# Expert tiles in one table and two lists, weight splits and scales inside attention, last rows routed among the tiles

## Chip, cores and metric

The kernel runs on one core of a Trainium2 chip. The metric is device time in microseconds (us) of one execution. The engines are TensorE (PE, with its weight loads PEld), VectorE (DVE), ScalarE (ACT), GpSimd (POOL) and SyncE (SP), each with an instruction queue of its own that runs in order; they wait for one another by semaphores.

## What is computed

The input is one image x of shape 1 x 64 x 128 x 128. First an attention block with a residual, then a mixture of experts with a residual:

```python
x = x + conv_ref(_ln_c(x), ...)          # per-pair layer norm, attention over the last axis, gate, projection
t = tokens(x)                            # 8192 tokens of 128 features
t = t + ffn_ref(_ln_t(t), ...)

# conv_ref: x = (x - mu) * rsqrt(var + eps) * ln_w + ln_b   (mean and variance over everything)
#   q, k, v, g = projections of 4 heads of 32; softmax(q k / sqrt(32) + bias) v, times sigmoid(g), times wrep
# ffn_ref: gate_logits = xf @ Wg + bg; top 2 of 8 experts, weights by a softmax over the two
for e in range(E):
    h = gelu(xf @ W1[e] + b1[e])         # 128 -> 512
    out = out + w_dense[:, e:e + 1] * (h @ W2[e] + b2[e])
```

The kernel computes an expert only for the tokens that chose it.

## The kernel before

The image lies in SBUF as 64 rows (HALF) of 128 tokens each: the partition is the channel and half, a row is a slice xt[:, i, :]. Three phases follow each other.

**Prologue.** SP and ACT each load one half: the x chunks, then the four chunks of ln_w, then the four of ln_b (`load_half`, L524 to L535). DVE computes row statistics in two chains of two chunks, prepares the projection weights (L925 to L934), gets the global scale, and multiplies and adds ln_w and ln_b chunk by chunk (L943, L949). PE computes the bias of attention from x1 (`bias_rows`, L1281) and transposes it.

**Attention.** 32 units of four rows run in a software pipeline of 35 steps (`attention_steps`, `step(s, p)` on every engine). Unit u is projected in step u, its logits and exponentials follow in steps u and u+1, its values in step u+2, its residual (L1011) in step u+3. The order on each engine is written out by hand. The routing of finished rows rides along: `plan()` says in which step statistics, row scales, normalised rows (POOL), transposes, gate logits (PE), picks and ranks of a batch happen. BATCHES are rows 0 to 15, 16 to 27, 28 to 39 and 40 to 63; only the first three are routed inside attention. POOL scatters each routed row of 128 tokens by an indirect DMA (L700), once for each of two choices, into a region per expert in HBM. `scatter_plan()` gives it at most 5 a step, 8 after step 31; twelve of batch 2 are left for after attention. ACT squares the expert weights in steps 32 and 33 (`weight_squares`, L824); DVE builds the first tile table in step 33 (`tile_table`).

**Between attention and tiles.** PE sums the squares (L1446), DVE gets the power-of-two scales (L1180 to L1190), then does statistics, scales and rows of batch 3 (L1061), b2 (L1197 to L1202), its logits, picks, ranks, positions and the second table, and two `split_weights` (L1207). ACT makes the high parts of the weights (L864), copies turned rows (L814) and the 24 late rows (L869). PE waits for table 2 and both splits before it starts the tile steps.

**Tiles.** The table has 78 tiles of 256 tokens in two parts: 2 * 40 * 128 / 256 + 7 = 47 for rows 0 to 39, and 31 for rows 40 to 63. A tile that isn't full is filled by padding rows, which SP writes (`pad_rows`) into the regions. SP loads a tile (`load_rows`, L589), eight buffers ahead. In step s PE transposes tile s+1 (L1473), multiplies tile s by W1 (L1483 to L1485, hidden layer in fp16 high and low parts), and tile s-1 by W2 (L1500). ACT makes fx_h, the Gelus (L887) and the weighted output yo of tile s-2 (L895). DVE makes the low parts (L1226) and the hidden high and low parts (L1232, L1234). POOL sends a tile with two indirect DMAs (L728). ACT may write yo of tile t only when tile t-4 is sent. Among the sends of the first 38 tiles POOL also scatters the 48 late rows. From step 54 on DVE adds first results to xt (`add_first`, L1248) in every second step. The steps 5 to 52 run in a loop of eight.

The lines that the steps below touch in PE's tile step, before:

```python
pe.wait_ge(table_ready, 2)
pe.wait_ge(w_split, 2)
tile_steps(pe, tile_step)
```

## Time and profile before

| | |
|---|---|
| median of 3 runs | 893.18 us |
| lowest, highest | 892.15, 895.83 us |
| profiled execution | 893.04 us, its span 891.3 us |
| PE / PEld / DVE busy | 77% / 63% / 73% of the span |
| ACT / POOL busy | 69% / 45% |
| mean granted clock of PE | 0.906 |
| HBM traffic | 70 GB/s over the span |

The span runs from the first to the last instruction; the device time has 1.7 us more. A line of the trace names the source line, the engine, the operation and out<-in, with a count and times. "idle before" is the engine's idle time just before, and what ended it. DMAs of a queue are issued in order and land later.

### The profile page before, as it was taken

What the parts mean: (1) busy time and instruction counts of PE and PEld (TensorE: products, weight loads), DVE (VectorE), ACT (ScalarE), POOL (GpSimd) and SP (SyncE); (2) the same over time, 40 slices, a digit from 0 to 9 for tenths busy, and PEclk for the clock granted to TensorE, in tenths of its full rate; (3) what the DMA queues carried; (4) which work ended last, traced back from release to release, by engine and by line L of the source; (5) the groups of instructions that cost most, each with busy time, mean ns of one, the idle gap of its engine ahead of it and who ended that gap; (6) DMA issues with size and microseconds to landing.
All of it is one profiled execution on the core that took longest, in us unless ns stands there. A gap on an engine that the chain in (4) does not pass through costs nothing.

```text
span 891.3 us, 23217 instructions
## 1 busy us (share of the span) xinstructions
PE 686.5 (77%) x7225; PEld 559.9 (63%) x7226; DVE 650.3 (73%) x2359; ACT 615.3 (69%) x1548; POOL 405.4 (45%) x469
## 2 busy tenths in 40 slices
PE   0089999997996889678977635299888888999980
PEld 0088777775775667557856425278666766888860
DVE  3983688887778667877677584778666766799974
ACT  0862899996996669568866652078766676888860
POOL 5000122223433256346553760047777777666661
PEclk9999999998998879879988755599999999999995
DMA  9959200000000001000100132113333223434457
GB/s 215 259 124 201 56 3 2 2 2 1 2 2 2 1 16 32 4 7 26 32 26 16 46 88 57 43 50 82 90 83 86 84 81 93 154 97 143 150 159 256
DMA packets 65923, 63.98 MB, mean 72 GB/s; under 512 B 21157, under 2 KB 57062, under 8 KB 64296
## 3 DMA queue, kind: packets, MB, share of 16 engines
q1 hardware_dynamic: 54168, 34.90, 15.9%
q0 software_dynamic: 9152, 18.76, 6.3%
q10 hardware_dynamic: 2512, 9.18, 3.8%
q8 instruction: 48, 0.79, 0.4%
q14 instruction: 43, 0.35, 0.1%
HBM read 35.88 MB, written 26.93 MB: 70 GB/s over the span
## 4 chain that ended last, share of the span: by engine, by line
PE 51%; DVE 17%; ACT 9%; POOL 8%; issue 7%; DMA 6%; SPq 1%; ACTq 0%; POOLq 0%; DVEq 0%
PE PT L1500 8%; PE PT L1338 6%; ACT L L801 5%; POOL expert_out L728 5%; DMA shared<-in_L_conv_ln_b 4%; PE B L1368 4%; PE S L1326 4%; POOL routed L700 3%; PE S L1483 3%; PE B L1281 3%; PE S L1485 3%; PE S L1484 3%; PE A L1293 2%; DVE xt L1011 2%; DVE pl L976 2%
## 5 line engine op out<-in xcount | busy, mean ns | idle before, releaser
L728 POOL DMA_INDIRECT expert_out<-yo,rows_all x156 | 157.4, 1009 | 87.1 <-ACT yo L895 49.7
L887 ACT ACTIVATE hf<-S,b_sb,inv_hscale 128x256 f32<-128x256 f32 x312 | 150.9, 564 | 47.4 <-PE S L1485 46.8
L801 ACT ACTIVATE L<-L,lmin 128x128 f32<-128x128 f32 x512 | 159.4, 392 | 0.4
L700 POOL DMA_INDIRECT routed<-pay,pos x128 | 125.1, 977 | 69.9 <-issue 34.6
L989 DVE CUSTOM_DVE_ANT_0 L<-S,biasN 128x128 f32<-128x128 f32 x512 | 117.3, 284 | 16.3 <-issue 15.1
L684 POOL TENSOR_TENSOR og<-on,rden 128x256 f32<-128x256 f32 x64 | 39.4, 617 | 193.0 <-DVE on L1002 134.1
L1234 DVE SCALAR_TENSOR_TENSOR hl<-hf,hscale,hh 128x512 f16<-128x512 f32 x156 | 117.8, 755 | 5.5
L1232 DVE TENSOR_SCALAR hh<-hf,hscale 128x512 f16<-128x512 f32 x156 | 77.5, 497 | 54.0 <-ACT hf L887 53.9
L1483 PE MATMUL S<-fx_h,w_h 128*128 128x256 f16 x312 | 86.8, 278 | 11.1 <-issue 9.5
L796 ACT ACTIVATE ph<-PT 128x512 f16<-128x512 f32 x128 | 75.9, 595 | 25.5 <-PE B L1355 16.8
L1338 PE MATMUL PT<-identity,L 128*128 128x128 f32 x512 | 81.7, 296 | 10.1 <-ACT L L801 10.0
L976 DVE TENSOR_TENSOR pl<-PT,ph 128x512 f16<-128x512 f32 x128 | 84.2, 683 | 6.3 <-ACT ph L796 6.0
L1500 PE MATMUL PT<-w_h,hh 128*128 x624 | 86.6, 220 | 2.1 <-DVE hl L1234 1.8
L672 POOL TENSOR_TENSOR xs<-x,xs 64x512 fp32r<-64x512 f32 x32 | 40.6, 1268 | 103.4 <-ACT xs L777 67.1
L1484 PE MATMUL S<-fx_l,w_h 128*128 128x256 f16 x312 | 86.5, 277 | 0.0
L1485 PE MATMUL S<-fx_h,w_l 128*128 128x256 f16 x312 | 86.4, 277 | 0.0
L1500 PE MATMUL PT<-w_h,hl 128*128 x624 | 85.8, 219 | 0.0
L1500 PE MATMUL PT<-w_l,hh 128*128 x624 | 85.7, 219 | 0.0
L1326 PE MATMUL S<-qk_all 32*128 32x128 f32 x1024 | 78.2, 293 | 0.7 <-ACT qk_all L783 0.7
L1293 PE MATMUL A<-xs,w4h 128*128 128x512 f32 x64 | 46.0, 718 | 38.7 <-DVE vl L970 37.6
L1338 PEld LDWEIGHTS PT<-identity,L 128*128 128x128 f32 x512 | 62.9, 152 | 17.9 <-ACT L L801 12.2
L1326 PEld LDWEIGHTS S<-qk_all 32*128 32x128 f32 x1024 | 65.5, 195 | 8.1 <-issue 5.7
(238 smaller groups left out, 1738.4 us busy)
## 6 DMA issues: line engine op xcount, KB each, us to landing
rows_all<-routed SPq DMA_DIRECT2D x78, 130.0 KB
shared<-expert_out SPq DMA_DIRECT2D x6, 768.0 KB
shared<-in_L_ffn_W SPq DMA_DIRECT2D x8, 512.0 KB, 7.2
routed<-blank SPq DMA_DIRECT2D x30, 129.0 KB, 2.6
expert_out<-yo,rows_all POOLq DMA_INDIRECT x156
out<-xt SPq DMA_DIRECT2D x6, 384.0 KB
xt<-in_x SPq DMA_DIRECT2D x4, 512.0 KB, 14.3
xt<-in_x ACTq DMA_DIRECT2D x4, 512.0 KB, 9.8
```

Of the source, the lines that this page charges most:

```text
L700: pool.indirect_dma_start(routed[TABLE_OF[b]], bass.IndirectOffsetOnAxis(ap=pos[k][:, row:row + 1], axis=0), source[:, part_row(b, i), :], ...
L728: pool.indirect_dma_start(expert_out, bass.IndirectOffsetOnAxis(ap=row_place[t % IN_BUFS][:, k, W + 1:W + 2], axis=0), yo[t % YO_BUFS][:, ...
L801: last = nc.scalar.activation(L[p][:, h, i, :], L[p][:, h, i, :], ACT.Exp, scale=-1.0, bias=lmin[p][:, h * R + i:h * R + i + 1])
L887: last = nc.scalar.activation(hf[p][:, b, :], S[2 * p + pair][:, k * TILE:(k + 1) * TILE], ACT.Gelu, scale=inv_hscale[:, 0:1], bias=b1_fla ...
L989: last = nc.vector.tensor_tensor_reduce(out=L[p][:, h, i, :], in0=S[h][:, i * P:(i + 1) * P], in1=biasN[:, h, :], scale=-float(D) ** -0.5, ...
L1234: nc.vector.scalar_tensor_tensor(hl[p][:, b, :], hf[p][:, b, :], hscale[:, 2:3], hh[p][:, b, :], ALU.mult, ALU.subtract).then_inc(hl_ready, 1)
L1326: last = nc.tensor.matmul(S[h][:, c], q[d, c], k[d, c], start=True, stop=True)
L1338: last = nc.tensor.transpose(PT[i % 2][:, h * P:(h + 1) * P], L[p][:, h, i, :], identity[:])
L1483: nc.tensor.matmul(dst, w1_h[:, block_at], fx_h[p][:], start=True, stop=False)
L1484: nc.tensor.matmul(dst, w1_h[:, block_at], fx_l[p][:], start=False, stop=False)
L1485: last = nc.tensor.matmul(dst, w1_l[:, block_at], fx_h[p][:], start=False, stop=True)
L1500: last = nc.tensor.matmul(PT[p][:, k * P:(k + 1) * P], h_part[p][:, b, k * P:(k + 1) * P], w_part[:, block_at], start=False, stop=b == HB ...
```

## The change

- One table with 71 tiles replaces two tables with 78. It has two lists of eight experts: the tiles of rows 0 to 39 and those of rows 40 to 63, with one region per expert, so that late rows go on where the routed ones end. FULL = 33 tiles are sure to be full, and need neither padding nor the late rows. `full_table` (DVE, step 33) gives these 33; `rest_table_counts`, `rest_table` and `rest_table_rows` give the other 38 in tile steps 11 to 13.
- ACT squares the weights in eight blocks, two in each of the steps 17 to 20 (`SQUARES_STEP`); b1's square is made in step 24; PE sums them and DVE reads and makes the scales in step 25 (`SCALES_STEP`). ACT makes the high parts in steps 32 and 33, DVE the low parts in steps 33 and 34.
- PE, ACT and DVE start the tile steps once table 1 is there. In the tile steps come b2 (after step -1), row scales (0), late rows (1 to 3), their turns (2 to 7) and logits (3 to 8), picks (8, 9), ranks and positions (10). POOL scatters the 48 late rows from tile 8 to tile 28, SP pads the regions before load 29, and loads tile 33 once all is scattered.
- All tile steps are written out, no loop. The additions of first results come in two of three steps, from step 52.
- Scatters in attention: 6 a step, 8 in steps 22 to 24, 28 to 30 and after 31; second choices one step sooner.
- Prologue: ln_w and ln_b chunks are loaded in turns; three chains of row scales (chunk 0, chunk 1, chunks 2 and 3); weight preparation on ACT and POOL; the first product with ln_w ahead of the global scale.

```diff
+    ROUTED = sum(n for _, n in BATCHES[:3])
+    FULL = ROUTED - (E - 1)
+    TILES = 2 * HALF * P // TILE + E - 1
...
+        ADD_AT = {DONE + 5 + 3 * i // 2: divmod(i, 4) for i in range(12)}
...
+        SQUARES_STEP, SCALES_STEP = 17, 25
+        LATE_STEP = dict(rows=1, turns=2, picks=8, ranks=10)
...
-                quota = 5 if s < UNITS else 8
+                quota = 14 if s == LAST - 1 else 8 if s in (22, 23, 24, 28, 29, 30) or s >= UNITS else 6
...
             for c in range(CH):
                 engine.dma_start(lnw_at[c][k], lwv[f, :, chunk(c), :]).then_inc(lnw_in[c], 16)
-            for c in range(CH):
                 engine.dma_start(lnb_at[c][k], lbv[f, :, chunk(c), :]).then_inc(lnb_in[c], 16)
...
+            load_rows(0, FULL - IN_BUFS // 2)
+            pad_regions()
+            load_rows(FULL - IN_BUFS // 2, FULL)
+            sp.wait_ge(padded, 32 * PADS)
+            sp.wait_ge(table_ready, 2)
+            for k in range(2):
+                sp.wait_ge(scattered[3][k], 16 * BATCHES[3][1])
+            load_rows(FULL, DONE + IN_BUFS)
...
-            spread = PART_TILES[0] - 9
+            start, spread = LATE_STEP["ranks"] - 2, FULL - 4 - (LATE_STEP["ranks"] - 2)
...
+                if 0 <= s - SQUARES_STEP < HB:
+                    weight_squares(2 * (s - SQUARES_STEP))
+                    weight_squares(2 * (s - SQUARES_STEP) + 1)
+                if s in (UNITS, UNITS + 1):
+                    high_weights(s - UNITS)
...
+            def copy_late():
+                act.wait_ge(xn_ready, GROUPS)
+                nc.scalar.activation(pay[2][:, :, 0:W], pay[1][:, :, 0:W], ACT.Copy).then_inc(copied, 1)
...
+            tile_steps(tile_step, {LATE_STEP["turns"] + 1: copy_late, LATE_STEP["ranks"]: lambda: gate_exponential(3)})
...
+                if s == SCALES_STEP - 1:
+                    bias_squares()
+                if s == SCALES_STEP:
+                    weight_scales()
                 if s == UNITS + 1:
-                    tile_table(0, carry[3])
+                    full_table()
+                    split_weights(0)
+                if s == UNITS + 2:
+                    split_weights(1)
...
+            after = {-1: second_bias, 0: lambda: scale_rows(3), picked: lambda: pick(3, (0, 1)), picked + 1: lambda: pick(3, (2, 3)),
+                     placed: lambda: positions(3), placed + 1: rest_table_counts, placed + 2: lambda: held.extend(rest_table()),
+                     placed + 3: lambda: rest_table_rows(*held)}
+            for n in range(3):
+                after[LATE_STEP["rows"] + n] = lambda n=n: late_normal_rows(ROUTED // R + 2 * n, ROUTED // R + 2 * n + 2)
...
+                    if turned_at(s) - 1 in LATE_GROUPS:
+                        gate_logits(turned_at(s) - 1, S[2 * p + 1], 0)
+                    if turned_at(s) in LATE_GROUPS:
+                        turn_rows(turned_at(s), S[2 * p], pay[1])
+                    if s == LATE_STEP["ranks"]:
+                        rank(3, S[2 * p + 1], 0)
...
-            pe.wait_ge(table_ready, 2)
-            pe.wait_ge(w_split, 2)
-            tile_steps(pe, tile_step)
+            pe.wait_ge(table_ready, 1)
+            tile_steps(tile_step, {})
```

## Rows read from the trace of the kernel before

**Rows 1.** Busy us (x instructions) by stretch: PE, PEld, DVE, ACT, POOL; clock, DMA.
```profile
200.00:507.00 307.00, 246.56 (x2665) 197.29 (x2663) 228.33 (x1145) 229.23 (x610) 143.03 (x165) 0.88 0.05 15
507.00:575.00 68.00, 27.39 (x164) 21.89 (x163) 48.20 (x157) 19.29 (x16) 21.39 (x23) 0.53 0.24 60
575.00:742.60 167.60, 148.21 (x1615) 118.17 (x1616) 117.10 (x210) 119.51 (x292) 117.20 (x121) 0.97 0.29 80
742.60:857.00 114.40, 113.08 (x1329) 95.62 (x1327) 100.64 (x179) 95.84 (x237) 75.36 (x72) 1.00 0.45 137
```

**Rows 2.** Timeline (start us, us, what): PE's transposes of tiles 0 and 43.
```profile
574.95 0.45 PE L1473 MATMUL A<-identity,rows_all 128*128 128x128 f32 x1 [15.23 <-issue]
...
742.60 0.28 PE L1473 MATMUL B<-identity,rows_all 128*128 128x128 f32 x1
```

**Rows 3.** Timeline: POOL's first send of a tile.
```profile
588.62 0.96 POOL L728 DMA_INDIRECT expert_out<-yo,rows_all  x1 [21.09 <-ACT yo L895]
```

**Rows 4.** Timeline: VectorE in the prologue.
```profile
36.69 0.20 DVE L925 COPY gt<-bgrow 1x128 f32<-1x128 f32 x1
...
38.97 1.39 DVE L934 TENSOR_TENSOR w4l<-og,w4h 64x512 fp32r<-64x512 f32 x2
...
46.33 2.48 DVE L949 SCALAR_TENSOR_TENSOR x<-x,grstd,shared 128x1024 f32<-128x1024 f32 x2 [1.33 <-DMA shared<-in_L_conv_ln_b]
```

**Rows 5.** DMA issues by line, 8.15 to 8.30 us: KB each, us to landing.
```profile
shared<-in_L_conv_ln_w SPq DMA_DIRECT2D x1, 512.0 KB, 25.9
```

**Rows 6.** Timeline: ScalarE between steps 18 and 19.
```profile
295.36 2.44 ACT L801 ACTIVATE L<-L,lmin 128x128 f32<-128x128 f32 x8
297.70 0.37 ACT L789 ACTIVATE gt<-A 128x256 f32<-128x256 f32 x1
```

**Rows 7.** Groups by line and form, ScalarE, 498 to 517 us: busy, mean ns, idle before.
```profile
L824 ACT ACTIVATE w_h<-shared 128x4096 f16<-128x4096 f32 x2 | 7.2, 3606 | 0.0
```

**Rows 8.** Timeline: the residual, once a step, of steps 22, 23 and 32 to 34.
```profile
350.47 0.76 DVE L1011 SCALAR_TENSOR_TENSOR xt<-B,brep,xt 64x512 f32<-64x512 f32 x1 [1.01 <-PE B L1368]
365.81 0.74 DVE L1011 SCALAR_TENSOR_TENSOR xt<-B,brep,xt 64x512 f32<-64x512 f32 x1 [1.90 <-PE B L1368]
...
494.72 0.76 DVE L1011 SCALAR_TENSOR_TENSOR xt<-B,brep,xt 64x512 f32<-64x512 f32 x1 [0.50 <-PE B L1368]
509.37 0.74 DVE L1011 SCALAR_TENSOR_TENSOR xt<-B,brep,xt 64x512 f32<-64x512 f32 x1 [1.59 <-PE B L1368]
520.28 0.76 DVE L1011 SCALAR_TENSOR_TENSOR xt<-B,brep,xt 64x512 f32<-64x512 f32 x1
```

**Rows 9.** Timeline: first table, a weight split, SyncE's first eight loads.
```profile
514.26 0.16 DVE L1152 TENSOR_TENSOR counts<-carry,region_base 128x8 f32<-128x8 f32 x1
...
557.31 4.48 DVE L1207 SCALAR_TENSOR_TENSOR w_l<-shared,hscale,w_h 128x4096 f16<-128x4096 f32 x1
...
539.38 8.43 SPq L589 DMA_DIRECT2D rows_all<-routed  x8
```

**Rows 10.** Chain that ended last, 660 to 672 us: start us, us, what.
```profile
665.50 2.24 DMA expert_out<-yo,rows_all
...
668.46 2.34 DMA rows_all<-routed
...
670.84 0.44 PE A L1473 x2
```

**Rows 11.** Groups by line and form, VectorE, 740 to 857 us: the additions of results.
```profile
L1248 DVE SCALAR_TENSOR_TENSOR xt<-shared,y_scale,xt 128x768 f32<-128x768 f32 x11 | 11.1, 1011 | 0.0
```

**Rows 12.** Busy us by stretch, columns as rows 1: scales and rows; picks; ranks, positions.
```profile
525.90:536.35 10.45, 4.66 (x20) 3.85 (x20) 9.79 (x45) 7.64 (x4) 8.01 (x9) 0.50 0.35 92
552.50:557.40 4.90, 0.04 (x1) 0.05 (x2) 4.44 (x15) 0.42 (x1) 0.00 (x0) 0.50 0.00 0
561.70:565.80 4.10, 0.00 (x0) 0.00 (x0) 3.65 (x17) 0.00 (x0) 0.00 (x0) 0.50 0.00 0
```

**Rows 13.** Timeline: ScalarE at the first Gelu.
```profile
578.35 1.28 ACT L887 ACT_TABLE_LOAD   x1 [1.89 <-PE S L1485]
```

More of the change, by code:

```diff
@@ L592, in _, with pad_rows @@
-            pad_regions(0)
-            sp.wait_ge(padded[0], 32 * PADS)
+            def pad_rows(at, n):
+                where = routed[at].rearrange("(k p) w -> p k w", p=P)
+                sp.dma_start(where[:, :, 0:W + 1], blank[:]).then_inc(padded, 16)
+                sp.dma_start(where[:, :, W + 1:W + 2], pad_place[:, n, :].bitcast(F32).unsqueeze(2),
+                             allow_slow_non_contiguous=True).then_inc(padded, 16)
+            for n in range(E - 1):
+                pad_rows(slice(E * REGION + n * TILE, E * REGION + (n + 1) * TILE), E + n)
@@ new lines, in pad_regions, with load_rows @@
+            def pad_regions():
+                sp.wait_ge(counts_ready, 1)
+                for e in range(E):
+                    at = sp.value_load(count_at[0:1, e:e + 1], min_val=0, max_val=TOKENS)
+                    pad_rows(bass.ds(at + e * REGION, TILE), e)
+            def load_rows(first, stop):
+                for t in range(first, stop):
+                    wait(sp, y_sent[t % YO_BUFS], sent_count(t % YO_BUFS, t - IN_BUFS))
+                    at = sp.value_load(row_at[0:1, t:t + 1], min_val=0, max_val=E * REGION + (E - 2) * TILE)
+                    sp.dma_start(rows_in[t % IN_BUFS], routed[bass.ds(at, TILE)].rearrange("(k p) w -> p k w", p=P)
+                                 ).then_inc(rows_loaded[t % IN_BUFS], 16)
@@ L908, in _, with multiply_weights @@
             chain = Chain(dve, dve_step)
-            for b in range(2):
-                for c in (2 * b, 2 * b + 1):
+            def multiply_weights(c):
+                dve.wait_ge(rows_normal, c + 1)
+                dve.wait_ge(lnw_in[c], 32)
+                nc.vector.tensor_tensor(x1[:, chunk(c), :], x1[:, chunk(c), :], lnw_at[c], ALU.mult).then_inc(lnw_used, 1)
+            for first, stop in ROW_CHAINS:
+                for c in range(first, stop):
                     dve.wait_ge(x_in[c], 32)
@@ L914, in _ @@
                 chain.link(last)
-                k = slice(2 * b * CR, 2 * (b + 1) * CR)
+                k = slice(first * CR, stop * CR)
                 row_scales(chain, k, 1e-6)
@@ L1111, in positions @@
                 first, n = BATCHES[b]
-                rows, t = slice(first, first + n), TABLE_OF[b]
+                rows = slice(first, first + n)
                 a, c, f = r_a[:, 0:n, :], r_b[:, 0:n, :], posf[:, 0:n]
@@ L1209, in split_weights, with second_bias, late_normal_rows @@
                                                w_h[n][:].rearrange("p b e d -> p (b e d)"), ALU.mult, ALU.subtract).then_inc(w_split, 1)
-            for g in range(10, GROUPS):
-                take_logits(g, B)
-            pick(3)
-            split_weights(0)
-            take_ranks(3, B)
-            positions(3)
-            tile_table(1, carry[4])
-            split_weights(1)
+            attention_steps(step)
+            def second_bias():
+                dve.wait_ge(hscale_ready, 1)
+                chain.link(nc.vector.tensor_scalar(b2_row[:], b2_row[:], hscale[0:B2_ROWS, 1:2], hscale[0:B2_ROWS, 2:3], ALU.mult, ALU.mult))
+                b2_e = b2_row[:].rearrange("o (e d) -> o e d", e=E)
+                chain.link(nc.vector.tensor_copy(b2_parts[:], b2_e))
+                lo = slice(B2_ROWS - 1, B2_ROWS)
+                chain.link(nc.vector.tensor_tensor(b2_parts[lo], b2_e[lo], b2_parts[lo], ALU.subtract))
+                nc.vector.tensor_copy(ones_x[:], ones[0:B2_ROWS, :]).then_inc(b2_ready, 1)
+            def late_normal_rows(first, stop):
+                for g in range(first, stop):
+                    normal_rows(g)
             def tile_step(s, m, _=None):
@@ L1384, in gate_logits, with rank @@
                 for i in range(R):
-                    last = nc.tensor.matmul(bank[:, RANK_AT + i * E:RANK_AT + (i + 1) * E], xnT[:, i * P:(i + 1) * P], wg_sb[:],
+                    last = nc.tensor.matmul(bank[:, column + i * E:column + (i + 1) * E], xnT[:, i * P:(i + 1) * P], wg_sb[:],
                                             start=True, stop=True)
                 last.then_inc(lg_full, 1)
-            def rank(b, bank):
+            def rank(b, bank, at=RANK_AT):
                 n = BATCHES[b][1]
```

435 lines of the change are left out of this document (232 added, 203 removed).

## Prediction

> **What bounds the kernel now.** I read the stage table first [rows 1]: each engine's busy time by stretch. In the last 35 tiles TensorE is busy 113 of 114 us, but only 27 of the 68 us between 507 and 575, at a mean granted clock of 0.53: there weights are squared, scaled and split and rows 40 to 63 are routed, and no tile is computed. The first tile's transposes start at 574.95, those of tile 43 at 742.60 [rows 2]. Between them TensorE isn't the bound either: from the first send at 588.62 [rows 3] POOL issues 121 indirect DMAs in 154 us [rows 1], 1.27 us each without a rest, since the scatter of every late row (48) and every tile's two sends cost that much. The last 35 tiles and the tail take 891.3 - 742.6 = 148.7 us and change little. So four places are to be priced: prologue, attention, gap, and the tiles up to the last late scatter.
>
> **Prologue: -5 us.** VectorE does 3.7 us of weight preparation (36.69 to 40.36) ahead of its global statistic, then one product, then waits 1.33 us for the first ln_b chunk, until 46.33 [rows 4]. The change gives the preparation to ScalarE and POOL, which idle there, and issues ln_b 0 where ln_w 1 stands now: near 8.2, in 25.9 us [rows 5], so it lands at 34.1. First output of L949: 46.33 moves to about 41.3, and the small matmuls behind it with it. The third chain of row scales ends before it is needed: nothing.
>
> **Attention: +13.1 us.** (a) The squares move from steps 32 and 33 into steps 17 to 20, two blocks a step. In place of them come the scaled copies, as long: no gain there. ScalarE is tight where they are put: it ends eight exponentials begun at 295.36 and starts the gate at 297.70 without idle time [rows 6], and VectorE's chain hangs on the copy behind that gate. An operation of 128x4096 takes 3.61 us [rows 7], a quarter of it 0.90, with its fixed part and accumulator read 1.15, two a step 2.3. The step that carries a square today took 509.37 - 494.72 = 14.7 us, the next 10.9 [rows 8]: 3.8 for 3.8. Exposed: 4 x 2.0 = 8; bounds 0 and 10. (b) Scales in step 25: eleven chained VectorE operations of 0.2 us. A step with six pick operations took 365.81 - 350.47 = 15.3 us [rows 8], 4.4 over a plain one, more than the chain's own length, as TensorE idles and restarts slow. +3; bounds 1 and 4.4. (c) A matmul and its read in bank A, and b1's square: +0.8; bounds 0 and 1.5. (d) Scatters 6 and 8 a step for 5: in steps 25 to 27 POOL also normalises rows; one scatter, 1.27, comes through, and later steps have fewer: +1.3; bounds -1 and 4. With the prologue attention ends 8.1 later than now.
>
> **The gap: the first tile 21.8 us earlier.** VectorE's table starts at 514.26 and the residual behind it at 520.28 [rows 8, 9]: 6.0 us, now 4.5 with 33 entries for 47. Then the first weight split, 4.5 [rows 9], which the change puts ahead of the last residual and second choice (1.2 us). Second choice ends at 524.9, not 521.5: 3.4 later. Then, as now, 12 scatters and the loads at 539.38 [rows 9]: with 3.4 and 8.1, 550.9. Transposes start 2.3 us behind a load [rows 10]: 553.2. The second split hides behind the scatters. The padding of the regions leaves this path, as the first 33 tiles are full.
>
> **Tiles 0 to 32: the work of the gap comes back.** The late rows now go between tiles on VectorE. A plain tile costs it (100.6 - 11.1) / 34.8 = 2.6 us [rows 1, 11] of TensorE's 3.3, which leaves 0.7. Until the late positions are known (after step 10) it does: 5.7 us to the first hidden block, as now, which covers b2's four operations; 11 tiles, 28.3; row scales and 24 rows 10.45; logits 1.2; picks 4.9; ranks and positions 4.1 [rows 12]. Sum 54.7. Its waits: in steps 4 to 8 TensorE takes 3.3 + 1.4 for four fp32 transposes and the logits, against 2.8 on VectorE, 9.5 in all; partly at the same time ScalarE's copy of 24 rows, queued ahead of tile 5's fx_h, on which TensorE waits; rank matmuls 2.2; one restart at the half clock 1.1. The positions are ready 67.5 us after tile 0: 620.7. Bounds 58 and 73.
>
> POOL's first late scatter stands ahead of send 8 and waits for the positions with send 8 behind it, and ScalarE's output 12 waits for send 8. Then 48 scatters and sends 8 to 27: 88 x 1.27 = 111.8 us, to 732.5. Only then may SyncE load tile 33. From a POOL DMA at 665.50 to the transposes of the tile whose load waited for it it's 5.4 us [rows 10]: tile 33 at 737.9. TensorE, some six tiles ahead of the sends, runs dry about 10 us before. 38 tiles remain, where 35 remain at 742.60: 737.9 + 148.7 + 3 x 3.3 = 896.5, and +1.5 as the additions of first results, 1.01 us [rows 11], come in two of three tiles instead of one of two: 2.6 + 0.67 = 3.3, no room left. Span 898.0. The profiled run took 893.04 for its span of 891.3, the median is 893.18: with 1.7, 899.7, taken as 899.5. Seven tiles of 3.3 and the gap are gained, but 33 tiles now cover 185 us where 43 covered 168.
>
> The Exp of the late rows' gate stands between Gelus. The first Gelu's table load takes 1.28 us [rows 13], so two more cost ScalarE 2.6 in step 10, beside VectorE's ranks: about 0.5 on the path, inside the 67.5. The Trainium skill (ScalarE: Activation LUTs, What ACT_TABLE_LOAD costs) puts a switch at about 2.7 us with its drain, 5.3 for two, and so speaks against this placement.
>
> **Rivals.** (1) Faster: squares and scales hide in attention, where ScalarE is busy 229 of 307 us [rows 1]. Against it: the tight place above. If attention costs 2 for 13, and ScalarE's copy and the turned rows hide behind VectorE's own work (4.5): 899.5 - 11 - 4.5 = 884. It decides whether ScalarE comes to the gates of steps 18 to 21 with over 2 us in hand. (2) Half of it: (a) and (b) cost 6 for 11, the copy 2 less: 892.5. (3) The clock: each time TensorE runs dry (steps 2 and 10, before tile 33) it restarts at 1.2 GHz, as at 575; three restarts at 2 us more than counted, and 1 us in each square step: +10, 909. The 0.97 of that stage now [rows 1] speaks against. (4) Each of the two switches also empties ScalarE, for about the load's own length, in the one step where hidden blocks, ranks and gate meet: 2 x 1.28, so 902. This is what the skill's figure gives; the row has one load behind an idle time, and can't tell. That the tiles don't start at once is no case: table, first split and high parts are ready over 15 us before the loads.
>
> **Chances.** Forecast 0.42, of which 0.07 within the bound; (1) 0.25; (2) 0.12; (3) 0.13; (4) 0.08. A measurement can tell about 0.5%, 4.5 us, from no change. Faster 0.25; same 0.07 + 0.12 = 0.19; slower 0.35 + 0.13 + 0.08 = 0.56. The range goes from 881, rival (1) with its terms' lower bounds, to 910, rival (3); the forecast's own is 893 to 905.
>
> **What would show it.** Right: the first bias matmul near 42.7; steps 17 to 20 each 2 us longer and step 25 by 3; the first tile's transposes near 553; the last late scatter near 732, 180 us behind it; TensorE idle some 10 us before tile 33; then 3.3 us a tile. Wrong: steps 17 to 20 no longer than now (rival 1), a granted clock under 0.9 from tile 0 to 32 (rival 3), or a POOL that has pauses among the late scatters.

## The result, and the profile of the changed kernel

| | before | changed |
|---|---|---|
| median of 5 runs | 892.15 us | 905.33 us |
| lowest, highest | 890.92, 895.83 us | 905.00, 911.12 us |
| ratio of the changed to before | | 1.0151, 95% interval 1.013 to 1.0171 |
| profiled execution | span 891.3 us | 911.12 us, span 908.6 us |
| first tile's transposes | 574.95 | 557.10 |
| first, last late scatter | | 630.97, 742.99 |
| transposes of tile 33, from there to the end | | 748.79, 159.8 |

The kernel got slower by 1.5%. The direction is the one forecast (slower had a chance of 0.56), the size isn't: 899.5 against 893.2 us was 6.3 us more, and the medians differ by 13.2. By time alone the rivals at 902 and 909 us lie nearer to 905.3 than the forecast does, so only the rows can choose. The changed kernel's trace is of the slowest of its five executions (granted clock 0.883); the other four took 905.0 to 905.5 us with spans near 903.2 (0.897 to 0.901). About 5 us of what follows belong to that one execution, and I say where.

Stretches of the changed kernel, columns as in [rows 1]: attention, gap, tiles up to the first late scatter, late scatters, the last 37 tiles.

```profile
105.00:515.00 410.00, 335.94 (x3652) 269.39 (x3651) 302.40 (x1545) 322.24 (x855) 169.88 (x196) 0.89 0.04 13
515.00:557.00 42.00, 8.33 (x65) 4.25 (x64) 19.09 (x40) 5.99 (x5) 16.74 (x14) 0.54 0.07 22
557.00:631.00 74.00, 59.00 (x548) 49.47 (x549) 51.79 (x141) 42.59 (x91) 16.61 (x17) 0.85 0.16 43
631.00:749.00 118.00, 76.03 (x778) 59.41 (x777) 66.80 (x136) 57.65 (x143) 90.24 (x92) 0.85 0.28 82
749.00:870.00 121.00, 120.61 (x1393) 101.89 (x1393) 104.06 (x186) 100.34 (x248) 72.50 (x70) 0.98 0.41 123
```

In the third stretch POOL is busy 16.6 of 74 us: the engine that is the bound afterwards has nothing to do, since the positions aren't known. In the fourth it issues without a rest and TensorE works 76 of 118 us. Timeline of the prologue (start us, us, what):

```profile
40.81 2.48 DVE L973 SCALAR_TENSOR_TENSOR x<-x,grstd,shared 128x1024 f32<-128x1024 f32 x2
...
42.24 3.98 PE L1380 MATMUL B<-wb_sb,x 128*128 128x8 f32 x18 [5.21 <-DVE x L973]
```

46.33 [rows 4] has become 40.81 without a wait for ln_b. The gap: VectorE's two weight splits, POOL's first scatters of the last batch in attention, and TensorE's first tile:

```profile
527.49 4.46 DVE L1286 SCALAR_TENSOR_TENSOR w_l<-shared,hscale,w_h 128x4096 f16<-128x4096 f32 x1
...
533.07 4.48 DVE L1286 SCALAR_TENSOR_TENSOR w_l<-shared,hscale,w_h 128x4096 f16<-128x4096 f32 x1
...
533.44 4.98 POOL L719 DMA_INDIRECT routed<-pay,pos  x1 [9.71 <-DVE pay L1176]
538.73 0.96 POOL L719 DMA_INDIRECT routed<-pay,pos  x1 [0.30 <-issue]
...
557.10 0.66 PE L1567 MATMUL A<-identity,rows_all 128*128 128x128 f32 x2 [29.43 <-DMA rows_all<-routed]
```

The first scatter meets the second split and takes 4.98 us instead of 0.96; it ends 0.87 us behind the split (533.07 + 4.48 = 537.55). Next, the largest stall among the first tiles, between tiles 6 and 7 (584.7 to 597.8), on ScalarE and TensorE:

```profile
584.02 2.77 ACT L898 ACTIVATE pay<-pay 128x3072 f32<-128x3072 f32 x1 [4.07 <-DVE pay L1094]
586.70 0.36 ACT L906 ACTIVATE fx_h<-B 128x256 f16<-128x256 f32 x1
...
589.61 0.28 PE L1587 MATMUL S<-fx_h,w_h 128*128 128x256 f16 x1 [4.50 <-ACT xnT L837]
```

ScalarE waits 4.07 us for the last of the late rows, copies them for 2.77, and only then turns to fx_h and the turned rows that TensorE waits for. Last, the chain from the last late scatter to tile 33 (start us, us, what), and TensorE's row for it:

```profile
742.99 2.30 DMA routed<-pay,pos
...
746.48 2.27 DMA rows_all<-routed
748.79 0.69 PE B L1567 x2
...
748.79 0.69 PE L1567 MATMUL B<-identity,rows_all 128*128 128x128 f32 x2 [10.78 <-DMA rows_all<-routed]
```

### The profile page after: what moved, and what is told of

The parts are those of the page before. It is cut to its first block, busy times and chain, and to the rows that moved or that the text cites. A ratio compares the mean times of both kernels' runs of the same rounds, so it can differ in the third digit from the quotient of the medians.

```text
span 908.6 us, 21702 instructions
## 1 busy us (share of the span) xinstructions
PE 674.0 (74%) x6950; PEld 549.3 (60%) x6950; DVE 630.6 (69%) x2346; ACT 601.3 (66%) x1514; POOL 400.0 (44%) x450
## 3 DMA queue, kind: packets, MB, share of 16 engines
q1 hardware_dynamic: 44104, 31.97, 13.9%
## 4 chain that ended last, share of the span: by engine, by line
PE 46%; DVE 23%; ACT 10%; issue 7%; POOL 6%; DMA 5%; SPq 2%; ACTq 0%; POOLq 0%; DVEq 0%
PE PT L1613 7%; PE PT L1439 6%; ACT L L824 5%; PE B L1469 4%; POOL routed L719 4%; PE S L1427 3%; PE B L1380 3%; PE S L1587 3%; PE S L1589 2%; PE S L1588 2%; PE A L1392 2%; DVE xt L1035 2%; DVE hl L1325 2%; POOL expert_out L747 2%; DVE pl L1000 2%
## 5 line engine op out<-in xcount | busy, mean ns | idle before, releaser
L747 POOL DMA_INDIRECT expert_out<-yo,rows_all x142 | 144.9, 1020 | 118.2 <-ACT yo L927 87.6
L917 ACT ACTIVATE hf<-S,b_sb,inv_hscale 128x256 f32<-128x256 f32 x284 | 137.9, 565 | 44.3 <-PE S L1589 44.3
L824 ACT ACTIVATE L<-L,lmin 128x128 f32<-128x128 f32 x512 | 159.8, 392 | 0.5
L1013 DVE CUSTOM_DVE_ANT_0 L<-S,biasN 128x128 f32<-128x128 f32 x512 | 117.3, 285 | 17.7 <-issue 16.5
L1325 DVE SCALAR_TENSOR_TENSOR hl<-hf,hscale,hh 128x512 f16<-128x512 f32 x142 | 107.0, 754 | 5.1
L1587 PE MATMUL S<-fx_h,w_h 128*128 128x256 f16 x284 | 82.0, 289 | 15.2 <-DVE fx_l L1313 8.2
L1323 DVE TENSOR_SCALAR hh<-hf,hscale 128x512 f16<-128x512 f32 x142 | 69.7, 491 | 32.3 <-ACT hf L917 32.1
L1613 PE MATMUL PT<-w_h,hh 128*128 x568 | 80.5, 224 | 5.0 <-DVE hl L1325 4.7
L1589 PE MATMUL S<-fx_h,w_l 128*128 128x256 f16 x284 | 81.9, 288 | 0.0
L1588 PE MATMUL S<-fx_l,w_h 128*128 128x256 f16 x284 | 81.9, 288 | 0.0
L1439 PEld LDWEIGHTS PT<-identity,L 128*128 128x128 f32 x512 | 64.3, 155 | 26.5 <-ACT L L824 20.6
L1613 PE MATMUL PT<-w_h,hl 128*128 x568 | 80.0, 223 | 0.0
L1613 PE MATMUL PT<-w_l,hh 128*128 x568 | 79.8, 223 | 0.0
## 6 DMA issues: line engine op xcount, KB each, us to landing
xt<-in_x SPq DMA_DIRECT2D x4, 512.0 KB, 14.2
```

The source lines that it names most:

```text
L747: pool.indirect_dma_start(expert_out, bass.IndirectOffsetOnAxis(ap=row_place[t % IN_BUFS][:, k, W + 1:W + 2], axis=0), yo[t % YO_BUFS][:, ...
L824: last = nc.scalar.activation(L[p][:, h, i, :], L[p][:, h, i, :], ACT.Exp, scale=-1.0, bias=lmin[p][:, h * R + i:h * R + i + 1])
L917: last = nc.scalar.activation(hf[p][:, b, :], S[2 * p + pair][:, k * TILE:(k + 1) * TILE], ACT.Gelu, scale=inv_hscale[:, 0:1], bias=b1_fla ...
L1013: last = nc.vector.tensor_tensor_reduce(out=L[p][:, h, i, :], in0=S[h][:, i * P:(i + 1) * P], in1=biasN[:, h, :], scale=-float(D) ** -0.5, ...
L1325: nc.vector.scalar_tensor_tensor(hl[p][:, b, :], hf[p][:, b, :], hscale[:, 2:3], hh[p][:, b, :], ALU.mult, ALU.subtract).then_inc(hl_ready, 1)
L1439: last = nc.tensor.transpose(PT[i % 2][:, h * P:(h + 1) * P], L[p][:, h, i, :], identity[:])
```

## The experiments

All ran beside the kernel before; a ratio is to that, with its 95% interval, and a difference in us is a difference of ratios times 893. The other columns are from the traces, in us: the last residual of attention, the first tile's transposes, the first late scatter, tile 33's transposes.

| kernel | ratio | interval | residual | tile 0 | late | tile 33 | span |
|---|---|---|---|---|---|---|---|
| changed | 1.0151 | 1.0130-1.0171 | 532.0 | 557.1 | 631.0 | 748.8 | 908.6 |
| e1 | 1.0104 | 1.0077-1.0130 | 528.4 | 546.8 | 618.2 | 736.7 | 895.9 |
| e2 | 1.0123 | 1.0100-1.0146 | 527.0 | 548.0 | 623.7 | 742.7 | 901.8 |
| e3 | 1.0083 | 1.0047-1.0119 | 523.5 | 548.6 | 621.0 | 739.6 | 899.2 |
| e4 | 0.9928 | 0.9903-0.9953 | 516.2 | 570.9 | | | 886.8 |
| e5 | 1.0043 | 1.0027-1.0059 | 527.8 | 552.8 | 617.6 | 736.6 | 896.1 |
| e6 | 1.0076 | 1.0050-1.0102 | 526.8 | 551.8 | 624.0 | 736.2 | 895.5 |
| e7 | 0.9912 | 0.9894-0.9930 | 529.7 | 548.0 | 613.1 | 726.3 | 885.4 |
| e8 | 1.0126 | 1.0107-1.0145 | 529.6 | 554.7 | 624.2 | 742.5 | 902.2 |
| e9 | 0.9827 | 0.9793-0.9861 | 524.5 | 542.7 | 605.7 | 718.0 | 877.4 |
| e10 | 0.9817 | 0.9787-0.9846 | 527.8 | 539.9 | 603.2 | 715.7 | 873.5 |
| e11 | 0.9722 | 0.9694-0.9749 | 523.8 | 531.9 | 595.4 | 708.2 | 866.4 |
| e12 | 0.9700 | 0.9676-0.9723 | 519.7 | 527.6 | 591.1 | 703.8 | 863.7 |

e4 has the old order of tiles, so its last columns stay empty. From tile 33 to the end it is 158 to 160 us in all the others: what moves tile 33 moves the time. Steps of attention: column s is the time from the residual in step s to the residual in step s + 1.

| step | 17 | 18 | 19 | 20 | 24 | 25 | 26 | 27 | 28 | 29 | 31 | 33 |
|---|---|---|---|---|---|---|---|---|---|---|---|---|
| before | 20.0 | 15.8 | 18.8 | 11.9 | 15.7 | 11.7 | 13.3 | 11.7 | 15.9 | 15.2 | 10.2 | 10.9 |
| changed | 21.7 | 17.7 | 20.6 | 13.6 | 17.3 | 17.7 | 11.7 | 11.9 | 15.8 | 15.2 | 10.2 | 14.0 |
| e3 | 21.6 | 15.5 | 19.2 | 11.7 | 17.7 | 16.7 | 11.7 | 11.9 | 14.3 | 15.2 | 10.5 | 13.9 |
| e6 | 21.7 | 17.7 | 20.5 | 13.6 | 16.4 | 17.4 | 11.8 | 11.9 | 15.4 | 13.5 | 10.3 | 13.9 |
| e8 | 21.7 | 17.2 | 18.9 | 13.6 | 16.4 | 11.5 | 16.2 | 11.7 | 14.2 | 15.1 | 12.1 | 14.0 |
| e9 | 20.0 | 15.7 | 18.8 | 11.8 | 17.3 | 17.7 | 11.7 | 11.9 | 15.9 | 15.2 | 10.2 | 14.5 |
| e12 | 20.0 | 15.5 | 18.9 | 11.7 | 16.4 | 11.6 | 13.6 | 12.8 | 15.3 | 13.5 | 11.7 | 14.1 |

**e1: the second choice one step earlier.**

```diff
-  second_at.setdefault(min(s + 1, LAST - 1), []).append(b)
+  second_at.setdefault(min(s + 1, LAST - 2), []).append(b)
```

> The changed kernel with one move: the second choice of rows 28 to 39 (two VectorE operations that wait for POOL's first twelve scatters, issued by 513.1 in the changed kernel) stands at the end of step 33 instead of step 34, ahead of the table, the first weight split and the last residual. Theory (the chain second choice, twelve scatters, load sets the first tile, and each weight split holds up the one POOL scatter that meets it): the scatters begin near 523.8 instead of 533.4, two of them take about 5 us instead of 0.96, the last ends near 547 instead of 552.3, the first tile's transposes stand near 552 instead of 557.1, and the time falls by 5 us, to about 900. Rival A (the slow first scatter is a cost of its own, not of the split): only one takes 5 us, the first tile stands near 548, -9. Rival B (something else, weights or the table, sets the first tile): the scatters move and the first tile doesn't, 0.

Measured: -4.2 us; its interval touches that of the changed kernel. POOL's scatters of the last batch:

```profile
523.70 0.96 POOL L719 DMA_INDIRECT routed<-pay,pos  x1 [0.30 <-issue]
524.97 4.27 POOL L719 DMA_INDIRECT routed<-pay,pos  x1 [0.30 <-issue]
529.54 4.99 POOL L719 DMA_INDIRECT routed<-pay,pos  x1 [0.30 <-issue]
534.84 0.95 POOL L719 DMA_INDIRECT routed<-pay,pos  x1 [0.30 <-issue]
```

Two slow scatters, one for each split (splits 523.93 to 528.39 and 529.22 to 533.70), and none that is slow for being the first: rival A falls. The scatter at 523.70, begun 0.23 us ahead of the first split, took its 0.96. Tile 0 comes 18.4 us behind the last residual instead of 25.1, so rival B falls too.

**e2: the second split among the tiles.**

```diff
-                if s == UNITS + 2:
-                    split_weights(1)
...
                 nc.vector.tensor_copy(ones_x[:], ...).then_inc(b2_ready, 1)
+                split_weights(1)
```

> The changed kernel with the second weight split moved from behind the second choice to a place behind the first tile's low part and the second bias, where VectorE waits for the first hidden block. Theory (the split held POOL's first scatter for 4 us): that scatter takes 0.96 us, the loads come 4 us earlier, the first tile's transposes stand near 553 as first forecast; of the 4.5 us that the split now takes between tiles 0 and 1 about 2 are exposed, so the time falls by 2 (between -4 and +1). Rival (the scatter is slow by itself): the first tile stays at 557 and the time rises by 2 to 4.

Measured: -2.5 us. The first scatter took its plain time, and the split stands where VectorE waited:

```profile
528.41 1.01 POOL L719 DMA_INDIRECT routed<-pay,pos  x1 [9.70 <-DVE pay L1174]
...
552.87 4.47 DVE L1284 SCALAR_TENSOR_TENSOR w_l<-shared,hscale,w_h 128x4096 f16<-128x4096 f32 x1
```

Tile 0 comes 21.0 us behind the last residual instead of 25.1: the 4.1 us are the split's hold on POOL. From tile 0 to the first late scatter it is 75.8 us, so some of it is given back. The interval of the time touches that of the changed kernel; the rows are clearer than the time.

**e3: two of eight squares.**

```diff
-                if 0 <= s - SQUARES_STEP < HB:
-                    weight_squares(2 * (s - SQUARES_STEP))
-                    weight_squares(2 * (s - SQUARES_STEP) + 1)
+                if s == SQUARES_STEP:
+                    weight_squares(0)
+                    weight_squares(2 * HB - 1)
```

> The changed kernel with two of its eight squares of the weight blocks (the first of W1 and the last of W2, both in step 17); the other six are left out and ones stand for their sums, so the scales of the weights are other powers of two. Theory (ScalarE is tight where they were put, so each square of 1.03 us is exposed by about 0.9): steps 18 to 20 take 17.7 - 1.8, 20.6 - 1.8 and 13.6 - 1.7 us as in the kernel before, step 17 stays at 21.7, time -5.3. Rival 1 of the prediction (they hide in attention, and the longer steps have another cause): 0.

Measured: -6.1 us (interval some 4 wide to each side); steps 18 to 20 lost 2.2, 1.4 and 1.9, together 5.5, and step 17, which kept its two, stayed at 21.6. Two squares cost 1.4 to 2.2 us wherever they stand in these steps. Rival 1 of the prediction falls.

**e4: the kernel before with the new prologue.** The edit is the prologue's part of the diff above (load_half, ROW_CHAINS, the weight preparation on ScalarE and POOL, multiply_weights), put into the kernel before.

> The kernel before with the prologue of the changed one alone: ln_w and ln_b chunks in turns, row scales in three chains, the weight preparation on ScalarE and POOL. Theory: the first residual comes at 105.0 instead of 110.1, everything behind it moves with it, time 892.2 - 5 = 887. Rival (the 5 us are given back where other transfers or POOL's constants set the pace): between -2 and 0.

Measured: 886.29 us, -6.4 us; by the traces the last residual comes 4.1 earlier and the span is 4.5 shorter. The prologue alone beats both kernels.

**e5: the copy of the late rows later.**

```diff
-                    if k == 0 and i == 0:
+                    if k == 1 and i == 0:
                         pool.wait_ge(copied, 1)
...
-            tile_steps(tile_step, {LATE_STEP["turns"] + 1: copy_late, ...
+            tile_steps(tile_step, {LATE_STEP["ranks"] + 2: copy_late, ...
```

> The changed kernel with ScalarE's copy of the 24 late rows moved from behind tile step 3 to behind tile step 12; POOL waits for it ahead of the first scatter of the late rows' second choice instead of ahead of the first late scatter. Theory (the copy waits about 4 us for VectorE's last row, takes 2.8, and fx_h and the turned rows stand behind it, so that TensorE runs dry at tile 7 and restarts at the half clock): the 13.1 us between tiles 6 and 7 become about 6, the first late scatter comes 67 us behind tile 0 instead of 73.9, the time falls by 6 to 7. Rival (VectorE's own work, rows, picks and positions, sets the positions, and the copy lies beside it): the stall shrinks but the first late scatter moves by 2 at most, time -2 to 0.

Measured: -9.6 us by the ratios. Tile 7 follows tile 6 in 4.7 us instead of 13.1, and the first late scatter stands 64.8 us behind tile 0; in the changed kernel and in e1, e3, e6 and e8, which keep the copy, it is 69.5 to 73.9. The granted clock of that stretch differs too, so I compare at like clock: 71.4 us with the copy (e1, 0.88) against 64.8 and 65.0 without (e5 and e7, 0.89), and 69.5 with it (e8, 0.94) against 63.4 without (e10, 0.94). So 6 to 7 us of the path were this one operation, and its rival falls.

**e6: late scatters over fewer tiles, padding in pieces.**

```diff
-            start, spread = LATE_STEP["ranks"] - 2, FULL - 4 - (LATE_STEP["ranks"] - 2)
+            start, spread = LATE_STEP["ranks"] - 2, FULL - 7 - (LATE_STEP["ranks"] - 2)
...
-            load_rows(0, FULL - IN_BUFS // 2)
-            pad_regions()
-            load_rows(FULL - IN_BUFS // 2, FULL)
+            load_rows(0, FULL - 12)
+            for e in range(E):
+                load_rows(FULL - 12 + e, FULL - 11 + e)
+                pad_region(e)
+            load_rows(FULL - 4, FULL)
```

> The changed kernel with the 48 late scatters spread over sends 8 to 25 instead of 8 to 28, and the padding of the eight regions put singly between loads 21 to 29 instead of as one block ahead of load 29. Theory (POOL sets the pace until the last late scatter; tile 33 then needs that scatter and send 25): 84 indirect DMAs of 1.27 us from the first late scatter instead of 88, so tile 33 comes 5 us earlier, the 16.5 us stall at tile 29 goes and costs nothing of its own, time -5. Rival A (the stall at tile 29 is what makes tile 33 late): more than -8. Rival B (TensorE or the loads can't follow): 0.

Measured: -6.7 us; tile 33 stands 112.2 us behind the first late scatter instead of 117.8. In the changed kernel SyncE pads the regions in one block ahead of load 29, from 704.39 on:

```profile
704.39 0.41 SPq L575 DMA_DIRECT2D routed<-blank  x1
...
718.65 0.37 SPq L576 DMA_DIRECT2D routed<-pad_place  x1
719.96 29.35 SPq L594 DMA_DIRECT2D rows_all<-routed  x7
```

That made 16.5 us between the transposes of tiles 28 and 29, here 7.6. It was no cost of its own: the 5.6 us gained are the four DMAs fewer ahead of tile 33 (5.1), and rival A, which wanted more than 8, falls.

**e7: the three together** (e1, e5 and e6).

> The changed kernel with the second choice in step 33, the copy of the late rows behind tile step 12, and the late scatters over sends 8 to 25 with the padding spread among the loads. All three lie one behind the other on the same path by the theory, so they add: -4 (as measured for the first alone), -6.5 and -5, together -15.5 against the changed kernel, about 890, or 0.997 of the kernel before. If one of them only uncovers another limit, the sum falls short: 895 to 900.

Measured: 886.51 us, -21.3 us against the changed kernel, where the three alone add to -20.5, more than the -15.5 expected. They add, as operations one behind the other on one path do.

**e8: the scale chain in step 31.**

```diff
-        SQUARES_STEP, SCALES_STEP = 17, 25
+        SQUARES_STEP, SCALES_STEP = 17, 31
```

> The changed kernel with the matrix product of the square sums, its read and the eleven chained scale operations in step 31 instead of step 25 (b1's square stays in step 24). Theory (the price of 6.0 us in step 25, 1.6 of it given back in step 26, comes partly from what meets there: picks' batch, eight scatters and row normalisation on POOL, whose operations hold up one of the chain for 1.1 us): step 25 goes back to about 11.7, step 31 rises from 10.2 by 3, time -1.5 (0 to -2). Rival (a chain on VectorE costs the same wherever it stands): step 31 rises by 4.5 to 6, time 0.

Measured: -2.2 us, an interval that touches the changed kernel's. The residuals of steps 25 to 27, changed kernel and then e8:

```profile
404.83 0.74 DVE L1035 SCALAR_TENSOR_TENSOR xt<-B,brep,xt 64x512 f32<-64x512 f32 x1 [2.13 <-PE B L1469]
422.57 0.76 DVE L1035 SCALAR_TENSOR_TENSOR xt<-B,brep,xt 64x512 f32<-64x512 f32 x1 [2.77 <-PE B L1469]
434.30 0.74 DVE L1035 SCALAR_TENSOR_TENSOR xt<-B,brep,xt 64x512 f32<-64x512 f32 x1 [0.87 <-PE B L1469]
```

```profile
404.53 0.74 DVE L1035 SCALAR_TENSOR_TENSOR xt<-B,brep,xt 64x512 f32<-64x512 f32 x1 [1.28 <-PE B L1469]
416.04 0.76 DVE L1035 SCALAR_TENSOR_TENSOR xt<-B,brep,xt 64x512 f32<-64x512 f32 x1 [1.02 <-PE B L1469]
432.27 0.74 DVE L1035 SCALAR_TENSOR_TENSOR xt<-B,brep,xt 64x512 f32<-64x512 f32 x1 [0.88 <-PE B L1469]
```

Step 25 is 11.5 again, but step 26 rose from 11.7 to 16.2. Steps 25 and 26 together took 29.5 and now 27.7, against 25.0 before the change; step 31 rose by 1.9. So the chain costs 1.7 in one place and 1.9 in the other, by the traces, and the 2.7 us by which steps 25 and 26 are still over the kernel before belong to something else, the scatters (e12).

**e9: the squares where ScalarE idles.** ScalarE's two longest waits near steps 17 to 24, in e7's trace:

```profile
286.52 0.60 ACT L807 ACTIVATE qk_all<-A 128x512 f32<-128x512 f32 x1 [6.30 <-PE A L1394]
...
381.02 0.21 ACT L843 ACTIVATE gate_e<-key 128x12 f32<-128x12 f32 x1 [5.63 <-DVE key L1129]
```

```diff
                 unit(s, p, 2, high_p, 1)
+                if s == 24:
+                    for j in range(HB, 2 * HB):
+                        weight_squares(j)
...
                 unit(s, p, 1, exponentials, 0)
+                if s == 18:
+                    for j in range(HB):
+                        weight_squares(j)
...
-                if 0 <= s - SQUARES_STEP < HB:
-                    weight_squares(2 * (s - SQUARES_STEP))
-                    weight_squares(2 * (s - SQUARES_STEP) + 1)
```

> The kernel with the three edits together, and the eight squares moved to two places where its trace has ScalarE idle: W1's four in step 18 between the first exponentials and the copy of q (idle 6.30 us ahead of that copy), W2's four in step 24 ahead of the gate's exponential (idle 5.63 us). Four squares take about 4.7 us. Theory (a square costs what it pushes, not what it takes; in steps 17 to 20 it stood between exponentials with no idle time behind it): steps 17 to 20 lose their 1.7 to 1.9 each, steps 18 and 24 don't grow, time -6 to -7 against the three together, 0.984 of the kernel before. Rival (ScalarE's load as such is what attention pays for): 0.

Measured: 880.44 us, -7.6 us against e7. Steps 17 to 20 are those of the kernel before to 0.1 us, with all eight squares done, and the same two operations still wait:

```profile
283.91 0.60 ACT L807 ACTIVATE qk_all<-A 128x512 f32<-128x512 f32 x1 [3.01 <-issue]
...
373.20 0.21 ACT L843 ACTIVATE gate_e<-key 128x12 f32<-128x12 f32 x1 [1.07 <-DVE key L1132]
```

Of the 7.4 us by which the first late scatter moved, 5.4 are there at tile 0; the other 2.0 come behind it, where the granted clock is 0.93 for 0.89.

**e10: the last batch's scatters inside attention.** On top of e9: eight scatters are allowed in steps 27 and 31, and the second choices stand in steps 28 and 32.

```diff
-  quota = 14 if s == LAST - 1 else 8 if s in (22, 23, 24, 28, 29, 30) or s >= UNITS else 6
+  quota = 14 if s == LAST - 1 else 8 if s in (22, 23, 24, 27, 28, 29, 30, 31) else 6
...
+  second_at.setdefault(s + (s < UNITS), []).append(b)
```

> The last kernel with the scatters of rows 28 to 39 drawn forward: eight instead of six in steps 27 and 31, the second choice of batch 1 in step 28 and that of batch 2 in step 32, so that six of the last twelve scatters are issued in step 33 and six in step 34. Theory (the first tile waits for POOL's last scatter, 543.4 in the three together, 10 us behind the second split): the last scatter ends near 531, the first tile's transposes come 2.3 us behind a load near 533 to 535, where split and last residual are ready as well; 12 us earlier, time -10 to -12 as TensorE then starts all 71 tiles sooner; what may be lost: up to 3 us where eight scatters push POOL's gate in steps 27 and 31. Rival (the late rows' chain behind the first tiles, on VectorE and ScalarE, doesn't start sooner, as weights and last statistics are late): tile 0 moves, the first late scatter by half of it, -5.

Measured: -0.9 us, no difference by the intervals; tile 0 at 539.9 and not at 533 to 535. POOL's scatters and ScalarE's gate of step 28:

```profile
434.54 0.39 ACT L813 ACTIVATE gt<-A 128x256 f32<-128x256 f32 x1 [2.95 <-POOL og L704]
...
523.47 5.16 POOL L720 DMA_INDIRECT routed<-pay,pos  x1 [0.30 <-issue]
528.93 5.00 POOL L720 DMA_INDIRECT routed<-pay,pos  x1 [0.30 <-issue]
```

Only six scatters were left for the last step, but two of them met the splits, so the last one still waited for the second split's end (533.09). And the eight scatters of step 27 kept POOL from its gate until 433.83 (431.06 in e9, with six); ScalarE waited 2.95 us for it, and step 27 took 15.6 us instead of 11.9. The expectation had this second price as a loss, and the first not at all.

**e11: the second split behind the scatters.** On top of e9, with the last batch's second choice in step 32 and batch 1's left in step 29.

```diff
-  quota = 14 if s == LAST - 1 else 8 if s in (22, 23, 24, 28, 29, 30) or s >= UNITS else 6
+  quota = 14 if s == LAST - 1 else 8 if s in (22, 23, 24, 28, 29, 30, 31, 32) else 6
...
+  second_at.setdefault(s + (b < 2), []).append(b)
...
-                if s == UNITS + 2:
-                    split_weights(1)
...
-            after = {-1: second_bias, 0: lambda: scale_rows(3), ...
+            after = {0: lambda: scale_rows(3), ...
...
             statistics(GROUPS - 1)
+            second_bias()
+            dve.wait_ge(scattered[2][1], 16 * BATCHES[2][1])
+            split_weights(1)
             tile_steps(tile_step, after)
```

> The kernel with squares in idle places, with these edits: the second choice of rows 28 to 39 at the end of step 32 and twelve scatters of it in steps 33 and 34 (eight instead of six in step 31; batch 1's second choice stays in step 29, where it costs nothing), the second bias in the wait behind attention, and the second weight split behind the landing of the last of these scatters. Theory (in the kernel before this one both splits met scatters and took 5.16 and 5.00 us of POOL's time, so that moving the scatters forward gained only 2.8 us at tile 0; and a second choice that waits for scatters of the same step cost 3.7 us in step 28): step 28 is 11.9 again, one scatter of about 5 us instead of two, the last scatter ends near 528 and the first tile's transposes stand near 533 instead of 542.7, the first low part near 535 behind the split; time -8 to -10 against the kernel with squares in idle places, 0.973 of the kernel before. Rival (the tiles behind give it back, as their order of work on VectorE is what sets the late rows): tile 0 moves by 9, the first late scatter by less than 5, time -4.

Measured: 868.0 us, -9.4 us against e9. One scatter is held (by the first split), and the second split and tile 0 follow the last of them:

```profile
519.45 5.16 POOL L720 DMA_INDIRECT routed<-pay,pos  x1 [0.30 <-issue]
...
528.55 4.48 DVE L1288 SCALAR_TENSOR_TENSOR w_l<-shared,hscale,w_h 128x4096 f16<-128x4096 f32 x1
...
531.88 0.66 PE L1572 MATMUL A<-identity,rows_all 128*128 128x128 f32 x2 [12.53 <-DMA rows_all<-routed]
```

Tile 0 moved by 10.8 and the first late scatter by 10.3: what is gained at tile 0 arrives, and the rival falls. The expectation named a wait of the second choice as the cause of the 3.7 us that it calls step 28's (27 in the table); the rows of e10 show POOL's gate behind eight scatters instead. With six scatters and the old place of the second choice it is 11.9 again; this run doesn't part the two.

**e12: scales in step 31 and five scatters.** On top of e11, with e8's line and

```diff
-  else 8 if s in (22, 23, 24, 28, 29, 30, 31, 32) else 6
+  else 8 if s in (22, 23, 24, 28, 29, 30, 31, 32) else 5 if s in (25, 26, 27) else 6
```

> The last kernel with the scale chain in step 31 and five scatters instead of six in steps 25 to 27 (five instead of two in step 28). With the scales alone moved, steps 25 and 26 together took 27.7 us where the kernel before takes 25.0. Theory (POOL's scatters and row normalisation push the gate of steps 25 and 26): with five scatters they take 25 to 26, step 31 stays 1.9 longer, time -1.5 to -4 against the last kernel. Rival (six scatters cost no more than five there, and the 2.7 us are the second choice's place): 0 to -1, within the interval.

Measured: 866.22 us, -2.0 us against e11, within the intervals. Steps 25 and 26 together take 25.2 (27.7 in e8), step 27 takes 1.1 more than in e8: one scatter fewer is worth 2.5 us in two steps. The second choice of rows 16 to 27 stands in step 29 in both, so the rival falls; the squares stand elsewhere than in e8, but in e9 that left steps 25 and 26 as they were. It is the fastest version, 3% below the kernel before. Its stretches from tile 0 to tile 33:

```profile
528.00:591.00 63.00, 51.62 (x544) 44.17 (x542) 49.13 (x136) 40.18 (x90) 16.82 (x16) 0.94 0.18 50
591.00:704.00 113.00, 79.20 (x779) 61.01 (x780) 67.11 (x138) 60.64 (x144) 86.40 (x88) 0.90 0.29 83
```

## Why the prediction was right, and where it was off

The sign and the sum's structure held. Two terms failed, each by an operation that I had called hidden or partly hidden, and in the other four executions of the changed kernel a third, too high, probably offsets half of them. Point by point:

**Prologue, -5: right.** First residual 105.0 for 110.1, first bias matmul 42.24 for the 42.7 named. e4 shows it alone.

**Attention, +13.1: met in the trace of the changed kernel, too high by 4 to 5 in two others.** The first table begins at 522.9, 8.6 behind 514.26 [rows 9], for the 8.1 forecast. In e5 and e6, whose attention has the same instructions, it begins at 518.7 and 517.7. Five of the later steps (24, 28, 29, 30, 32) are shorter in e6 by 0.4 to 1.7 us, each at a higher granted clock. The largest difference is that of step 29, in the changed kernel and in e6 (columns as above, the clock third from the end):

```profile
462.10:477.30 15.20, 12.03 (x119) 9.13 (x119) 10.80 (x56) 10.41 (x29) 7.57 (x9) 0.84 0.05 18
```

```profile
460.00:473.50 13.50, 9.93 (x120) 8.02 (x119) 10.82 (x55) 9.94 (x28) 6.37 (x7) 1.00 0.05 15
```

By terms: (a) squares 8, measured 7.1 (1.7, 1.9, 1.8, 1.7), shown by e3 and e9; the reason given, that ScalarE had no idle time behind its exponentials there, is what e9 turned round. The sum's second support, 3.8 us more in the step that carries a square, was a misreading: the step of 10.9 us (509.37 to 520.28 [rows 8]) carries the other square:

```profile
512.08 3.61 ACT L824 ACTIVATE w_h<-shared 128x4096 f16<-128x4096 f32 x1
```

(b) Scales 3: step 25 came out 6.0 longer, twice as much as named, and the chain's own part is 1.7 to 1.9 (e8). (d) Scatters 1.3, measured 2.5 in steps 25 and 26 (e12 against e8). Steps 24 to 27 of e6 take 57.5 us against 52.4, and these 5.1 are the sum of (b) to (d), but only because (b) was too high and (d) too low: luck.

**The gap: the step "the second split hides behind the scatters" failed.** It cost 4.0 us in POOL's first scatter (0.96 to 4.98), shown by e1, e2 and e11. Tile 0 came at 557.1 for 553.2. In e5, e6 and e8 it stands at 552.8, 551.8 and 554.7: there a cheaper attention pays for the split, and the forecast number is met, or nearly, for the wrong reason. The working has a slip as well: 4.5, 4.5 and 1.2 us behind 514.26 end at 524.5, not 524.9, so the second choice was to end 3.0 us later, not 3.4.

**From tile 0 to the positions, 67.5: mis-sized.** Measured 73.9, outside the bounds of 58 and 73; in the kernels with the same order (e1, e3, e6, e8) 69.5 to 72.3. The step that failed is the wait that I called "partly at the same time", ScalarE's copy ahead of fx_h: at like clock it costs 6 to 7 us (e5, e7 and e10 against e1 and e8). Without it the positions come 64.8 behind tile 0 (e5), 2.7 under the forecast, which had a part of it in. The sum had also one restart at the half clock, 1.1 us; up to 4.4 us of this stretch go with the clock, as rival (3) below shows.

**Then 111.8 us of POOL, 5.4 to tile 33, TensorE dry for about 10: right.** Measured 112.0, 5.8 and 10.78. From tile 33 to the end 159.8 for 160.1. In sum for the trace shown: 3.9 + 6.4 + 0.2 + 0.4 - 0.3 = 10.6 = 908.6 - 898.0. The other four executions are only 5.2 us over the span of 898.0. No trace of them is kept; if they spent attention as e5 and e6 did, a term that was 4 to 5 too high hid half of the two that were too low, and that the median fell so near the forecast is luck.

**The rivals.** (1) and (2), squares hidden: fell by steps 17 to 20 and by e3, although the idle time in which they could hide was there, in other places (e9). (3), the clock: not refuted. Its sign, a granted clock under 0.9 from tile 0 to 32, is there (0.85 in both stretches). Among kernels with the same instructions from tile 0 to the positions, the stretch takes 69.5 us at a clock of 0.94 (e8), 71.4 at 0.88 (e1), 72.2 at 0.83 (e6) and 73.9 at 0.85 (changed). Between tiles 6 and 7, where TensorE idles 4.5 us in both, the changed kernel and then e8 show:

```profile
584.70:597.80 13.10, 8.60 (x56) 7.10 (x54) 5.73 (x12) 8.61 (x17) 3.04 (x3) 0.70 0.12 32
```

```profile
582.30:593.10 10.80, 6.30 (x56) 4.82 (x54) 4.85 (x11) 8.60 (x17) 2.09 (x2) 0.84 0.09 26
```

So in the trace shown up to 4.4 us of this stretch and 4 to 5 of attention go with the clock. e8 has its 0.94 with the copy and the split in place, so a high clock doesn't need them moved, and the 0.94 of e12 doesn't show what starts the low one. Why one execution keeps the low level longer than another behind the same stall stays open, and no run parts the clock's price from that of the stalls. (4), table switches that empty ScalarE: fell. ScalarE around step 10, and POOL's first late scatter:

```profile
620.06 1.28 ACT L842 ACT_TABLE_LOAD   x1
621.35 0.22 ACT L842 ACTIVATE gate_e<-key 128x24 f32<-128x24 f32 x1
...
627.85 1.28 ACT L917 ACT_TABLE_LOAD   x1 [0.73 <-PE S L1589]
...
630.97 0.96 POOL L719 DMA_INDIRECT routed<-pay,pos  x1 [12.44 <-DVE pay L1163]
```

The first load begins as the output before it ends (620.04), and the exponential is done 7 us before VectorE wants it; the second delays a Gelu while VectorE works on positions. The Trainium skill (ScalarE: Activation LUTs, What ACT_TABLE_LOAD costs) has 2.7 us for a load with its drain; here no drain shows beside the 1.28.

## What to carry to other kernels

Ask of an operation that is put "into idle time" what stands behind it in its own queue. Eight squares cost 7.1 us between exponentials and nothing in front of two operations that waited 6 us anyway; one copy of 2.8 us, put ahead of what TensorE needed, cost more than twice its length. If work comes back on VectorE or POOL, count the time in which either keeps the other from starting, for each pair that can meet. And where a later stage is bound by an engine (here POOL's issues), look at what that engine does in the stage before: it idled 57 of 74 us there, so its first input is worth its whole delay.
